# A graph network kernel: part of the last product made during the last edge pass, and added by an identity product

## The reference

```python
feats = [node_features]
x = gcn_conv(x, src, dst, W1, b1, n)              # 256 -> 128
x = jax.nn.relu(batch_norm(x, g1, be1))
feats.append(x)
x = gcn_conv(x, src, dst, W2, b2, n)              # 128 -> 64
x = jax.nn.relu(batch_norm(x, g2, be2))
feats.append(x)
cat = jnp.concatenate(feats, axis=1)              # 256 + 128 + 64 = 448 columns
return jax.nn.relu(cat @ Wfc + bfc)               # 448 -> 256
```

## Time and profile before

| what | value |
|---|---|
| runs | 8927.5, 8935.06, 8939.72 us; median 8935.06 |
| span of the profiled execution (the only time its page gives for it) | 8929.5 us |
| PE busy | 66% of the span |
| POOL busy | 67% |
| DVE busy | 65% |
| ACT busy | 51% |
| last edge pass, first gather to last gather's start | 7742.0 to 8779.3 us |
| final product's stage, first PE instruction to the end | 8815.0 to 8929.5 us |

### The profile page before, as it was taken

One profiled execution on the slowest core, in us unless ns is written; L12 is line 12 of the kernel. 1 busy time (PEld: TensorE's weight loads), 2 busy tenths in 40 slices (PEclk: granted clock), 3 DMA queues, 4 the chain that ended last, 5 costly groups with the idle time before them and its releaser, 6 DMA issues. The chain is left out here.

```text
span 8929.5 us, 139064 instructions
## 1 busy us (share of the span) xinstructions
PE 5901.4 (66%) x32642; PEld 4121.6 (46%) x32642; DVE 5834.8 (65%) x17509; ACT 4580.0 (51%) x14026; POOL 5943.1 (67%) x6034
## 2 busy tenths in 40 slices
PE   5786567877688788477776788888864444433336
PEld 3443345554455555344443455555553333333335
DVE  8998788888599888566666688998862222211113
ACT  6897533333377676233333377777743333333332
POOL 7897377776577675177774266666647777577773
PEclk9998877777587777777777888898875555555557
DMA  1333244454244443244443366666612222111111
GB/s 47 112 116 106 73 131 137 133 135 111 67 106 106 114 100 88 73 133 132 132 132 103 131 176 177 178 180 178 176 64 53 53 53 53 39 27 27 27 27 40
DMA packets 518718, 903.15 MB, mean 101 GB/s; under 512 B 149411, under 2 KB 258877, under 8 KB 517564
## 3 DMA queue, kind: packets, MB, share of 16 engines
q0 software_dynamic: 226304, 550.69, 23.4%
q1 hardware_dynamic: 291644, 343.69, 12.7%
HBM read 820.41 MB, written 73.07 MB: 100 GB/s over the span
## 5 line engine op out<-in xcount | busy, mean ns | idle before, releaser
L1324 POOL DMA_INDIRECT all_Y<-table,all_row x3328 | 3270.9, 983 | 1450.5 <-issue 977.6
L1898 POOL DMA_INDIRECT all_Y<-table,all_row x1664 | 1570.0, 944 | 549.6 <-issue 506.4
L1914 PE MATMUL g1e_ps_u<-all_Y,g1e_onehot 128*128 128x128 f32 x1664 | 428.6, 439 | 618.0 <-DMA all_Y<-table,all_row 460.5
L1377 PE MATMUL be_ps_u<-all_Y,be_onehot 128*128 128x258 f32 x1664 | 665.1, 558 | 252.8 <-DVE all_acc L1612 246.5
L1914 PE MATMUL g2e_ps_u<-all_Y,g2e_onehot 128*128 128x64 f32 x1664 | 406.5, 426 | 639.5 <-DMA all_Y<-table,all_row 566.7
L1942 DVE TENSOR_TENSOR all_acc<-all_acc,g1e_ps_u 128x128 f32 x832 | 238.7, 287 | 809.8 <-PE g1e_ps_u L1914 703.6
L1942 DVE TENSOR_TENSOR all_acc<-all_acc,g2e_ps_u 128x64 f32 x832 | 183.6, 221 | 864.5 <-PE g2e_ps_u L1914 758.1
L1377 PE MATMUL a1e_ps_u<-all_Y,a1e_onehot 128*128 128x264 f32 x1664 | 708.7, 556 | 4.4 <-DVE all_acc L1612 2.7
L1914 PEld LDWEIGHTS g1e_ps_u<-all_Y,g1e_onehot 128*128 128x128 f32 x1664 | 370.3, 327 | 676.1 <-issue 350.4
L1914 PEld LDWEIGHTS g2e_ps_u<-all_Y,g2e_onehot 128*128 128x128 f32 x1664 | 370.5, 328 | 675.5 <-issue 348.7
L1377 PEld LDWEIGHTS be_ps_u<-all_Y,be_onehot 128*128 128x128 f32 x1664 | 407.2, 272 | 476.0 <-issue 345.2
(11 more groups left out here) (557 smaller groups left out, 15956.6 us busy)
## 6 DMA issues: line engine op xcount, KB each, us to landing
all_Y<-table,all_row POOLq DMA_INDIRECT x4992, 2.5
a1e_place_row<-places_dst SPq DMA_DIRECT2D x104, 256.0 KB
a2e_place_row<-places_dst SPq DMA_DIRECT2D x104, 256.0 KB
be_place_row<-places_src SPq DMA_DIRECT2D x104, 256.0 KB
te_place_row<-places_src SPq DMA_DIRECT2D x104, 256.0 KB, 4.1
all_Y<-lows_dst SPq DMA_DIRECT2D x98, 256.0 KB
all_Y<-codes_dst SPq DMA_DIRECT2D x98, 256.0 KB
all_acc<-lows_src SPq DMA_DIRECT2D x98, 256.0 KB
```

Source lines behind the costliest of these rows:

```text
L1324: pool.indirect_dma_start(out=rows[:, r, k, :], out_offset=None, in_=table, in_offset=bass.IndirectOffsetOnAxis(ap=order.row[:, t * 8 + k: ...
L1377: pe.matmul(ps_u[k % 4][:, 0:R], onehot[b][:, k, :], rows[:, t % RING, k, WEIGHT0:value_c0 + HC] if dot else summand[:, b, k, :], start=Tr ...
L1898: pool.indirect_dma_start(out=rows[:, r, k, :], out_offset=None, in_=table, in_offset=bass.IndirectOffsetOnAxis(ap=order.row[:, t * 8 + k: ...
L1914: last = pe.matmul(ps_u[u][:, k * width:(k + 1) * width], onehot[b][:, k, :], rows[:, r, k, :], start=True, stop=True)
```

## The change

Three things are done to the last edge pass and the final stage.

- A new class `Beforehand` gives the pass `g2e` extra steps. For window w, PE turns x after batch 2w (`turn`), ACT copies both halves out of PSUM in one instruction (`copy`), PE multiplies them and T1 with their 384 rows of Wfc after batch 2w+1 (`product`, three calls), and DVE copies the 128 x 256 result from PSUM into SBUF (`keep`). The results stay on the chip: 39 windows in the unused part of `acc`, 3 in `order.begins`, 8 in a new tile `rest`.
- The three weight DMAs are issued by SP at the start of `g2e`.
- The final stage makes two products for each window: T2 with its 65 rows of W, and an identity matrix with the kept result, which adds it in PSUM. Its turning and its copies are gone.

```diff
+class Beforehand:
+    def turn(self, pe, w):
+        wait(pe, self.s_turned, w - 1)
+        for k in range(2):
+            last = pe.transpose(self.ps_t[w % 2][:, k * P:(k + 1) * P], self.x[:, w, k * P:(k + 1) * P], self.c.ident[:, :])
+        last.then_inc(self.s_t, 1)
+    def copy(self, act, w):
+        act.wait_ge(self.s_t, w + 1)
+        wait(act, self.s_product, w - 1)
+        act.activation(self.turned[:, w % 2, :, :].rearrange("p k e -> p (k e)"), self.ps_t[w % 2][:, 0:2 * P], ACT.Copy).then_inc(self.s_turned, 1)
+    def product(self, pe, w):
+        if w == 0:
+            pe.wait_ge(self.s_weights, 16 * len(self.loads))
+        pe.wait_ge(self.s_turned, w + 1)
+        wait(pe, self.s_kept, w - 1)
+        to = self.ps_o[w % 2][:, 0:D]
+        for k in range(2):
+            pe.matmul(to, self.turned[:, w % 2, k, :], self.weights[k], start=k == 0, stop=False)
+        pe.matmul(to, self.first[:, w * P:w * P + P], self.weights[2], start=False, stop=True).then_inc(self.s_product, 1)
+    def keep(self, dve, w):
+        dve.wait_ge(self.s_product, w + 1)
+        dve.tensor_copy(self.room(w), self.ps_o[w % 2][:, 0:D]).then_inc(self.s_kept, 1)
...
+        def window_at(t, ahead):
+            w = (t - ahead) // 2
+            return w if early is not None and t >= ahead and (t - ahead) % 2 == 0 and w < NW else None
...
+                    if window_at(t, 0) is not None:
+                        early.turn(pe, window_at(t, 0))
+                    if window_at(t, 1) is not None:
+                        early.product(pe, window_at(t, 1))
...
+                    if window_at(t, MARKS) is not None:
+                        early.copy(act, window_at(t, MARKS))
...
+                    if window_at(t, 2) is not None:
+                        early.keep(dve, window_at(t, 2))
...
-                        first=Step(sources=[(x3, 0, P), (x3, P, P)], weights=[W[:, 0, :], W[:, 1, :]], width=256, relu=True,
-                                   direct=((T1, P, W[:, 2, :]), (T2, 65, W[:, 3, :]))))
+                        first=Step(sources=[], weights=[], width=256, relu=True,
+                                   direct=((lambda w: T2[0:65, w * P:w * P + P], lambda w: W[0:65, 3, :]), (lambda w: c.ident[:, :], room))))
```

More of the change, by code:

```diff
@@ L1868, in _, with __init__, load, sum_pass @@
                         dve.tensor_copy(beside.stepped[:, a0:a1], ps[:, 0:a1 - a0])
-def sum_pass(nc, c, stage, order, table, width, acc, spare):
+class Beforehand:
+    def __init__(self, nc, c, m, x, first, weights, loads, room):
+        self.c, self.x, self.first, self.weights, self.loads, self.room = c, x, first, weights, loads, room
+        self.turned = m.sb("turned", [P, 2, 2, P])
+        self.ps_t = [m.ps(f"ps_t{b}", [P, 512]) for b in range(2)]
+        self.ps_o = [m.ps(f"ps_o{b}", [P, 512]) for b in range(2)]
+        self.s_weights, self.s_t, self.s_turned, self.s_product, self.s_kept = (m.sem(x) for x in ("weights", "t", "turned", "product", "kept"))
+    def load(self, sp):
+        for to, frm in self.loads:
+            sp.dma_start(to, frm).then_inc(self.s_weights, 16)
+    def turn(self, pe, w):
[19 more added lines that the diff above has]
+        dve.tensor_copy(self.room(w), self.ps_o[w % 2][:, 0:D]).then_inc(self.s_kept, 1)
+def sum_pass(nc, c, stage, order, table, width, acc, spare, beforehand=None):
     RING, AHEAD, MARKS, U = 6, 4, 4, 4
@@ L1891, in sum_pass, with _ @@
         with nc.Block() as block:
+            if early is not None:
+                @block.sync
+                def _(sp):
+                    early.load(sp)
             @block.gpsimd
@@ L2065, in dense_chain @@
             K1, width1 = len(A.sources), A.width
-            turned1 = m.sb("turned1", [P, 2, K1, P])
+            turned1 = m.sb("turned1", [P, 2, max(K1, 1), P])
             ps_t1 = [m.ps(f"ps_t1{b}", [P, 512]) for b in range(2)]
@@ L2163, in product1 @@
                     if w == 0:
-                        pe.wait_ge(s_weights, 16 * len(weights))
+                        wait(pe, s_weights, 16 * len(weights))
                         if A.ones_row:
                             pe.wait_ge(s_ones, 1)
-                    pe.wait_ge(s_turned1, w + 1)
+                    if A.sources:
+                        pe.wait_ge(s_turned1, w + 1)
                     wait(pe, s_added, w - 1)
@@ L2172, in product1 @@
                                          stop=k == K1 - 1 and not A.direct)
-                    for k, (y, n, of) in enumerate(A.direct):
-                        last = pe.matmul(ps_o1[w % 2][:, 0:width1], y[0:n, w * P:w * P + P], of[0:n, 0:width1], start=False, stop=k == len(A.direct) - 1)
+                    for k, (left, right) in enumerate(A.direct):
+                        last = pe.matmul(ps_o1[w % 2][:, 0:width1], left(w), right(w), start=k == 0 and not A.sources, stop=k == len(A.direct) - 1)
                     last.then_inc(s_product1, 1)
@@ L2203, in _ @@
                 for t in range(STEPS):
-                    if A is not None and is_window(t - T1):
+                    if A is not None and A.sources and is_window(t - T1):
                         turn1(t - T1)
@@ L2826, in gnn_kernel @@
         turned_norm(nc, c, "g2l", 128, acc, dinv_of, T1, (g_b1, g_g1, g_be1), g_w2, tables[64], 64)
-        sum_pass(nc, c, "g2e", order, tables[64], 64, acc, T2)
-        turned_norm(nc, c, "n2", 64, acc, dinv_of, T2, (g_b2, g_g2, g_be2), ones_row=True)
         with ExitStack() as st:
```

17 lines of the change are left out of this document (15 added, 2 removed).

## The result

The changed kernel takes 8881.01 us (median of 4 runs, 8870.67 to 8885.04), against 8932.17 us for the kernel before beside it (4 runs); the ratio is 0.9947 [0.9933, 0.9961], so it is faster, by 35 to 60 us. Measured once more beside 15 runs of before, it took 8885.45 us (5 runs), ratio 0.9948 [0.9935, 0.9962].

What follows compares the result with a forecast made beforehand. POOL's gathers were taken to bound the last edge pass, PE the final stage. Edge pass cost 0; 5.2 us at the start plus 37.8 in 49 steps saves 43.0: 8935.06 - 43.0 = 8892 us, range 8882 to 8913.

Steps and rivals of the forecast that it cites:

- The edge pass costs nothing: Last edge pass: added work hides behind POOL's gathers and the ring of six batches; cost 0, bounds 0 to 21 us.
- Rival 2: Edge pass: DVE's added copies lengthen POOL's gathers, 21 us given back, time 8913 us; chance 0.05.
- Rival 3: Edge pass: POOL waits for PE and the kernel gets slower, each batch pair growing 1.2 us or more; chance 0.03.
- a chain that holds PE: Edge pass, turning to copy to product: holding 6 us per product gives 8942 us, at 7 us 8960 us.
- The start of the final stage: Weights already loaded, product 0 starts at 8814.97, first add near 8817.0 instead of 8822.25: 5.2 us gained.
- DVE becomes the bound: Final stage: DVE replaces PE as bound, 5.84 us per group of five windows against 9.73; 37.8 us saved in 49 steps.
- The handshake over two tiles: Final stage: with two PSUM tiles, a product starts 0.15 us after the add two windows back ended.
- Rival 4: Final stage: DVE alone fills it and little changes; even at 7.5 us per group 27 us won, 8908 us; chance 0.04.
- The clock: Final stage: PE's clock rises between 8818.5 and 8822 and stays full; rival, half clock throughout, 8919 us, chance 0.09.
- `bl`: Earlier chain with 256-column products where PE waits for DVE in every window; its clock stayed 1.00, PE busy 15.2 of 20 us.
- The tail, the root and the stores: Final stage: 11.9 us after the last add in both kernels, root no new wait, DMA busy a third of the time.
- the spread of the runs: 12 us between three runs, used with the DVE floor to set the range's low end at 8882 us.

Runs made afterwards that it cites:

- the second profile: The changed kernel measured again with no edit: 8885.45 us, ratio 0.9948; from `g1e` on 2238.6 us.
- Two edits aimed at the two parts: Changed kernel with ACT scaling four of five windows: 8880.86 us; with four PSUM tiles instead of two: 8876.85 us; with both: 8870.60 us.
- two of the variants: Changed kernel at a slower hour, identity product left out: 10,628.61 us; T2's product made twice: 10,710.94 us (kernel before then: 10,699.76 us).

## Why the prediction was right, and where it was off

**The edge pass costs nothing.** Right, and by its reason: POOL's gathers are the pace (944 ns, 1.25 us apart), and the early work alone changes the total by 0.9994. PE was forecast at 11.0 of 20 us and has 10.93 in the window from 7745 to 7765 at clock 0.50, 10.5 on average at 0.54; ACT's copy took 0.37 us against 0.4, DVE's 0.42 as said. Rival 2 (copies lengthen gathers) has gone: PSUM copies leave them at 944 ns, SBUF copies add 3 ns on average, 27 to the gathers beside them. Rival 3 (PE becomes what POOL waits for) needed twice PE's work by the prediction's count; the run with the product made five times comes to 21.4 of 20 us at half clock, and nothing moved. That count itself was too severe, since it held the clock at 0.50. Its prices for a chain that holds PE (50 us at 6 us, 68 at 7) don't come out of it either: two holds of 6 us beside 11.0 of work would make a pair of batches 23 us, 150 us for the pass. Neither the forecast nor the range rests on them.

**The start of the final stage.** Forecast 5.2 us gained, with the first add 2.07 us behind PE's first instruction; measured 2.08 us and 5.2. The stage as a whole begins 0.4 us later behind the last gather.

**DVE becomes the bound.** Right: forecast 5.84 us for a group and 57.6 for the adds, measured 5.76 and 56.8. The terms were each a little large: DVE alone was put at 5.6 and is 5.43 where four tiles let it run, since a plain step takes 0.66 us and not 0.68, and shift and scaling 1.05 and not 1.12. The handshake over two tiles, put at 0.24, is 0.33. That the second profile's 57.6 us of adds is the forecast to the tenth is luck: its groups are 5.76 too, and a later rise of the clock fills up the rest. Two edits aimed at the two parts took 0.65 us (scaling) and 0.33 us (tiles) from a group, and 0.99 together. Rival 4 (DVE needs 7.5 us or more) has gone.

**The clock.** It was forecast by `bl` to stay full although PE waits; it is 1.00 from 8820 on, and two records start 0.43 us behind the two before them from 8811.7 on, where it was 0.85, 5.7 us behind the first instruction (6.8 in the second profile), inside the forecast of 3.5 to 7. That half clock can last through this stage two of the variants show; this kernel shows it in neither of its profiles.

**The tail, the root and the stores.** 11.8 us against 11.9; DVE waits for POOL's root once, 1.3 us, in the last group; DMA is busy 0.31 to 0.38.

**The sum and the range.** 43.0 us forecast; 42.5 measured in the stretches that the change touches, and both comparisons of totals hold it (35 to 60 us, 34 to 58). What was off is the step from there to a number and a range: "the spread of the runs (12 us between three)". Three runs said too little of how much the untouched stages vary from one execution to the next: between the changed kernel's own two profiles the start up to `g1e` differs by 23.1 us, and over ten profiles by 26, while the low end at 8882 left 10 us for that. Of the 11 us between 8892 and 8881.01, 2.9 are that the kernel before took 8932.17 beside it and not 8935.06; the rest is of the size of that variation. That the gain in totals came out at 51 us beside a change of 42.5 is such variation too; the repetition, with 45.4, lies nearer.

## What to carry to other kernels

Work that is ready early belongs in a stage whose pace is set by an engine that it doesn't use, if a ring lies between the two; the stage by windows shows how much room there is, and here the pass held the product made five times over. When a bound engine is relieved, work out the next engine's own time for a period and the handshake between them separately: here they were 5.43 and 0.33 us, and each could then be lowered by itself. A change of half a per cent is judged by stretches between marks in two traces, not by the totals, whose untouched part varied by 26 us between profiles; and where the clock rises once in a stage, by the periods behind that rise.

## What the runs showed of the hardware

- PE can be busy in every microsecond and stay at 1.2 GHz: 125 us of the final stage with T2's product doubled, against 1.00 with the identity product doubled, which is as many records. The cause is open.
- PE's granted clock rose in the pass with more work on it: 0.50 before, 0.54 with the early product, 0.76 with it five times over. These are means; single records there run at one of the two levels (in the last of these runs two product calls took 1.71 us from 8115.32 on and 0.86 from 8117.52 on).
- At one hour a chip ran every kernel about 20% longer, with pauses of PE called issue in the edge passes, and at a later hour the same chip ran at the usual pace.
- DVE copies within SBUF touched POOL's gathers little: 946 ns against 943 on average, 0.968 us against 0.941 for those beside copies.
- PE's clock rose 5.7 us behind the final stage's first instruction in one execution of the changed kernel and 6.8 in another, which moved the stretch from its first to its last add by 0.7 us.
